# Low parts of expert weights made on GpSimd in the second routing front, and gathers that wait for the token list alone

## The reference, cut to what matters

```python
x = x + attention(layernorm(x))
x = x + mixture_0(layernorm(x))          # 4 experts, hidden 512, one shared expert
x = x + rwkv(layernorm(x))
x = x + mixture_1(layernorm(x))          # 8 experts, hidden 256, biases

# mixture_1
logits = x @ gate_w.T + gate_b
top_vals, top_idx = top_k(logits, 2)
routing = softmax(top_vals)
for e in range(8):
    h = x @ w1[e].T + b1[e]
    y = h[:, 0::2] * sigmoid(1.702 * h[:, 0::2]) * (h[:, 1::2] + 1.0)
    out += (y @ w2[e].T + b2[e]) * sum(routing * (top_idx == e))
```

## Time and profile before

| | |
|---|---|
| median of 3 runs | 743.87 us (743.05 to 746.04) |
| profiled execution, its own time | 742.95 us |
| its span in the trace | 741.1 us |
| PE busy | 660.9 us (89%) |
| DVE busy | 519.2 us (70%) |
| ACT busy | 349.6 us (47%) |
| POOL busy | 338.2 us (46%) |
| second front, from the first instruction to the first `up` | 577.4 to 608.4 us |
| expert phase of the second mixture, from the first `up` | 608.4 to about 714 us |

### The profile page before, as it was taken

The page is one execution under the profiler, slowest core; times in us unless marked ns, Lnnn a source line. Parts: engine busy times, 40 slices in busy tenths (PEclk is TensorE's granted clock), DMA queues, the critical chain, the costliest instruction groups (busy, mean ns, idle before and its releaser), DMA issues. The chain is left out here.

```text
span 741.1 us, 13768 instructions
## 1 busy us (share of the span) xinstructions
PE 660.9 (89%) x4339; PEld 538.2 (73%) x4339; DVE 519.2 (70%) x1087; ACT 349.6 (47%) x735; POOL 338.2 (46%) x326
## 2 busy tenths in 40 slices
PE   8889999889899999999994799999998589999950
PEld 6656666468788888888883688888887257888840
DVE  6778888957854465444442679999883778888847
ACT  2667777736403333333332365555462654555530
POOL 5977777410033433444213245555442065777530
PEclk9999999989999999999998799999987799999985
DMA  6800000110011311111103942000010012333229
GB/s 205 322 1 3 1 2 15 44 34 29 1 35 44 115 51 58 58 53 57 36 29 108 354 152 98 1 0 1 30 53 33 0 54 81 99 98 101 80 80 309
DMA packets 37186, 54.23 MB, mean 73 GB/s; under 512 B 6645, under 2 KB 28919, under 8 KB 36983
## 3 DMA queue, kind: packets, MB, share of 16 engines
q1 hardware_dynamic: 27832, 31.78, 12.8%
q0 software_dynamic: 7104, 19.41, 8.3%
q10 hardware_dynamic: 2176, 2.10, 0.9%
HBM read 37.28 MB, written 15.99 MB: 72 GB/s over the span
## 5 line engine op out<-in xcount | busy, mean ns | idle before, releaser
L1888 PE MATMUL banks<-r_xt,r_w_mixed 128*128 128x256 f32 x384 | 87.6, 388 | 1.4 <-ACT r_xt L1980 1.4
L1888 PEld LDWEIGHTS banks<-r_xt,r_w_mixed 128*128 128x128 f32 x384 | 73.9, 194 | 12.7 <-ACT r_xt L1980 2.1
L1567 DVE SCALAR_TENSOR_TENSOR f0x_s<-f0x_th,banks 128x512 f32<-128x512 f32 x35 | 24.1, 688 | 83.1 <-ACT f0x_th L1526 83.1
L1427 POOL DMA_INDIRECT f_y<-f0x_yout,f_slot_of x35 | 34.6, 987 | 99.4 <-ACT f0x_yout L1542 99.4
L1413 POOL DMA_INDIRECT f0x_xg<-f_xn,f_token_of x35 | 35.0, 999 | 66.0 <-DVE f_slot_of L1045 49.5
L1526 ACT ACTIVATE f0x_th<-banks 128x512 f32<-128x512 f32 x35 | 21.0, 600 | 86.8 <-PE banks L1478 86.8
L659 DVE TENSOR_REDUCE a_ssum<-a_e 128x6 f32<-128x1536 f32 x32 | 56.0, 1748 | 3.8 <-ACT a_e L526 3.6
L1478 PE MATMUL banks<-f_w_hi,f0x_xt_hi 128*128 x140 | 55.4, 396 | 0.9 <-ACT f0x_xt_hi L1517 0.9
L1478 PE MATMUL banks<-f_w_lo,f0x_xt_hi 128*128 x140 | 55.6, 397 | 0.0
L1413 POOL DMA_INDIRECT f1x_xg<-f_xn,f_token_of x39 | 40.8, 1045 | 32.4 <-DVE f_slot_of L1045 19.3
L1478 PE MATMUL banks<-f_w_hi,f0x_xt_lo 128*128 x140 | 55.2, 394 | 0.0
(11 more groups left out here) (357 smaller groups left out, 1885.4 us busy)
## 6 DMA issues: line engine op xcount, KB each, us to landing
f_w_lo<-in_f_w13T SPq DMA_DIRECT2D x4, 2048.0 KB, 12.0
r_y<-f_y SPq DMA_DIRECT2D x16, 256.0 KB, 5.2
f_w_lo<-in_f_w2T SPq DMA_DIRECT2D x4, 512.0 KB, 15.0
f_xn<-f_rows_normed SPq DMA_DIRECT2D x8, 256.0 KB, 2.1
f_b<-in_f_b SPq DMA_DIRECT2D x1, 2048.0 KB, 9.8
f_w_lo<-in_f_w2T SPq DMA_DIRECT2D x2, 1024.0 KB, 11.6
f_xn<-r_y SPq DMA_DIRECT2D x8, 256.0 KB
f1c_y<-f_y SPq DMA_DIRECT2D x8, 256.0 KB, 7.3
```

The source lines that it names most:

```text
L1427: pool.indirect_dma_start(k.y_dram, bass.IndirectOffsetOnAxis(ap=k.slot_of[:, done:done + 1], axis=0), yout[:, done % YB, :], None).then_i ...
L1567: dve.scalar_tensor_tensor(out=s1[:, t % 2, :], in0=th[:, t % 2, :], scalar=1.0, in1=glu_part, op0=ALU.add, op1=ALU.mult).then_inc(s1_done, 1)
L1888: last = pe.matmul(bank(1 + kind)[:, eb * T:(eb + 1) * T], r.w_mixed[:, kind, j // KB, j % KB, eb * P:(eb + 1) * P], xt[:, b % 2, j % KB, ...
```

## The change

In the second front the low parts of the four down units, and of the first three of the eight up units, become GpSimd subtractions of 128 x 1024 numbers, in front of the gathers in GpSimd's queue. TensorE's `take_left`, the negated identity and ScalarE's copies out of PSUM go. VectorE keeps five up units (3 to 7). `weigh` moves from the end of VectorE's queue to a place behind `experts`. `rows` is cut into `tokens` and `slots`, with one low unit (3) between the two and four behind. TensorE gets products whose result nobody reads (`keep_clock`), 14 behind the counts and 8 behind the lists. In both mixtures the gathers wait for `tokens_known` and `planed`, and `slots_known` is waited for in front of the first scatter. In the first front the order of VectorE's steps stays.

```diff
+        k.tables_read = (self.planed, 1)
...
-    def rows(self):
+    def tokens(self):
         dve.wait_ge(t.named, 1)
         then(dve.tensor_scalar(k.token_of[:], t.named_psum, float(TOK), None, ALU.add))
+        k.tokens_known = (t.step, self.done)
+
+    def slots(self):
         then(dve.scalar_tensor_tensor(out=t.unused[:], ...
         dve.wait_ge(t.planed, 1)
...
-        k.rows_known = (t.step, self.done)
+        k.slots_known = (t.step, self.done)
...
-    AT_ROWS, BEFORE_LIST = 2, 2
+    ON_SIDE, BEFORE_SLOTS = 3, 4
+    k.up_known = ((k.hi_done, k.up_parts), (side_low, ON_SIDE), (k.lo_done, k.up_parts - ON_SIDE))
...
     def _(pool):
         rank.clear(pool)
-        pool.memset(neg_ident[:], 0.0).then_inc(neg_zero, 1)
-        pool.wait_ge(neg_zero, 1)
-        pool.affine_select(out=neg_ident[:], ...
+        for n, (hi, lo) in enumerate(down_parts):
+            pool.wait_ge(down_high, n + 1)
+            pool.tensor_tensor(lo, f32(lo), f32(hi), ALU.subtract).then_inc(down_low, 1)
+        for n in range(ON_SIDE):
+            hi, lo = parts[n]
+            pool.wait_ge(k.hi_done, n + 1)
+            pool.tensor_tensor(lo, f32(lo), f32(hi), ALU.subtract).then_inc(side_low, 1)
...
     def _(pe):
+        def keep_clock(times):
+            for _ in range(times):
+                pe.matmul(m.banks[:, 7, 0:2 * P], m.ones[:], m.neg_half[:, 0:2 * P], start=True, stop=True)
         rank.count(pe)
-        pe.wait_ge(neg_ready, 1)
-        for n in range(BEFORE_LIST):
-            take_left(n)
+        keep_clock(14)
         rank.list(pe)
-        for n in range(BEFORE_LIST, len(down_parts)):
-            take_left(n)
+        keep_clock(8)
...
     def _(act):
         down_to_high(2)
-        down_to_low(0)
         down_to_high(3)
-        take_high(0)
-        down_to_low(1)
+        for n in range(4):
+            take_high(n)
         rank.negate(act)
-        for n in range(1, 5):
+        for n in range(4, k.up_parts):
             take_high(n)
-        down_to_low(2)
-        for n in range(5, k.up_parts):
-            take_high(n)
-        down_to_low(3)
...
     def _(dve):
         steps.experts()
-        for n in range(AT_ROWS):
+        steps.weigh()
+        steps.tokens()
+        for n in range(ON_SIDE, BEFORE_SLOTS):
             take_low(dve, n)
-        steps.rows()
-        for n in range(AT_ROWS, k.up_parts):
+        steps.slots()
+        for n in range(BEFORE_SLOTS, k.up_parts):
             take_low(dve, n)
-        steps.weigh()
...
-        pool.wait_ge(*k.rows_known)
+        pool.wait_ge(*k.tokens_known)
+        pool.wait_ge(*k.tables_read)
...
+                if done == 0:
+                    pool.wait_ge(*k.slots_known)
                 pool.wait_ge(y_done, done + 1)
...
                 if t == 0:
-                    pe.wait_ge(k.hi_done, k.up_parts)
-                    pe.wait_ge(k.lo_done, k.up_parts)
+                    for semaphore, value in k.up_known:
+                        pe.wait_ge(semaphore, value)
```

More of the change, by code:

```diff
@@ L1039, in rows @@
         then(dve.tensor_scalar(k.token_of[:], t.named_psum, float(TOK), None, ALU.add))
+        k.tokens_known = (t.step, self.done)
+    def slots(self):
+        t, dve, then, k = self.t, self.dve, self.then, self.k
         then(dve.scalar_tensor_tensor(out=t.unused[:], in0=t.named_psum, scalar=0.0, in1=t.neg_spare[:],
@@ L1075, in first_front @@
     parts, take_low = weight_units(v, k)
+    k.up_known = ((k.hi_done, k.up_parts), (k.lo_done, k.up_parts))
     k.all_known = ((k.hi_done, k.all_parts), (k.lo_done, k.all_parts))
@@ L1266, in second_front @@
     parts, take_low = weight_units(v, k)
-    AT_ROWS, BEFORE_LIST = 2, 2
+    ON_SIDE, BEFORE_SLOTS = 3, 4
     down_parts = parts[k.up_parts:]
-    down_high, down_left, down_low, neg_zero, neg_ready = (
-        sem(n) for n in "down_high down_left down_low neg_zero neg_ready".split())
+    down_high, down_low, side_low = (sem(n) for n in "down_high down_low side_low".split())
+    k.up_known = ((k.hi_done, k.up_parts), (side_low, ON_SIDE), (k.lo_done, k.up_parts - ON_SIDE))
     k.all_known = ((down_high, len(down_parts)), (down_low, len(down_parts)))
-    neg_ident = ctx.enter_context(nc.sbuf_tensor(f"{v.tag}r_neg_ident", [P, P], F32))
-    flat = lambda part: f32(part).rearrange("p e n -> p (e n)")
-    left = lambda n: (m.banks[:, 4:6, :] if n == 1 else m.banks[:, 6:8, :]).rearrange("p b n -> p (b n)")
     @block.gpsimd
@@ L1278, in _ @@
         rank.clear(pool)
-        pool.memset(neg_ident[:], 0.0).then_inc(neg_zero, 1)
-        pool.wait_ge(neg_zero, 1)
-        pool.affine_select(out=neg_ident[:], in_=neg_ident[:], compare_op=ALU.not_equal, fill=-1.0, base=0,
-                           pattern=[[-1, P]], channel_multiplier=1).then_inc(neg_ready, 1)
+        for n, (hi, lo) in enumerate(down_parts):
[5 more added lines that the diff above has]
+            pool.tensor_tensor(lo, f32(lo), f32(hi), ALU.subtract).then_inc(side_low, 1)
     @block.tensor
     def _(pe):
[L1286 to L1293, removed]
-            last.then_inc(down_left, 1)
+        def keep_clock(times):
+            for _ in range(times):
+                pe.matmul(m.banks[:, 7, 0:2 * P], m.ones[:], m.neg_half[:, 0:2 * P], start=True, stop=True)
         rank.count(pe)
-        pe.wait_ge(neg_ready, 1)
-        for n in range(BEFORE_LIST):
-            take_left(n)
+        keep_clock(14)
         rank.list(pe)
-        for n in range(BEFORE_LIST, len(down_parts)):
-            take_left(n)
+        keep_clock(8)
     @block.scalar
```

3 lines of the change are left out of this document (removed).

## The result

The changed kernel takes 751.80 us (median of 4 runs, 751.44 to 752.64), the kernel before 743.46 beside it (4 runs, 742.48 to 746.04). The ratio is 1.0109 with a 95% interval of 1.0084 to 1.0134: slower by about 8.3 us. Forecast were 751.2 us and "slower" as the likeliest case.

What follows compares the result with a forecast made beforehand. The chain of waits up to the first `up` was taken as deciding, with TensorE's expert phase unchanged. Ranking 12.7 us longer, stretch behind it 5.4 shorter: 743.87 + 7.3 = 751.2 us, range 739.0 to 754.5.

Steps and rivals of the forecast that it cites:

- The one number: Start of the first `up`, which all later work follows: forecast at 615.7, 7.3 us later than 608.39.
- What GpSimd gets: Seven subtractions of 128 x 1024 at 2.35 us each, upper bound 2.54, rounded output priced at nothing.
- The hold: In the ranking, GpSimd's SBUF reads hold off VectorE steps with two SBUF inputs, about 2.0 us per larger subtraction.
- The walk: Step-by-step pass through the ranking naming which VectorE steps wait, slip or pass: seven waits, together 12.7 us.
- What goes: Ranking's end to first `up`: `take_left`, ScalarE's copies and three VectorE subtractions go; 16.0 us becomes 10.6, 5.4 less.
- the gathers': Before the first `up`: second gather lands at about 614, before VectorE's last unit at 615.1, so costs nothing.
- The clock: TensorE's granted clock around the first `up`: 0 added, 1.5 us kept for the range if first tiles run at half speed.
- A: Rival: the two engines don't hinder one another; first `up` 5.1 us sooner, 4.6 put, 739.3 us; chance 0.29.
- B: Rival: the wait doesn't grow with subtraction size; 5.8 us on the ranking, time about 744; chance 0.13.
- C: Same mechanism in full: 2.54 us subtractions held to the end, 3.1 more plus clock 1.5, 754 to 756; within likeliest case's 0.58.
- The page's rule: SBUF contention between VectorE and GpSimd: whoever issues second is blocked fully; to the letter, about 2 us more.

Runs made afterwards that it cites:

- experiment 1: The changed kernel with the seven GpSimd subtractions waiting until the ranking's tables are written: 753.36 us, ratio 1.0136 to the kernel before.
- experiment 2: The changed kernel with each GpSimd subtraction replaced by two memsets, which read nothing (low parts zero): 739.40 us, ratio 0.9953 to the kernel before.
- experiment 3: The changed kernel with each GpSimd subtraction replaced by a one-input copy (low parts wrong): 742.53 us, ratio 0.9997 to the kernel before.
- 4: The changed kernel with each GpSimd subtraction cut into two of 128 x 512: 749.03 us, ratio 1.0080 to the kernel before.
- 5: The changed kernel with only the four down units on GpSimd and all eight up units on VectorE: 748.52 us, ratio 1.0065 to the kernel before.
- 7: The kernel before with only the gathers' wait changed, to the token list and the plane instead of the slots: 742.72 us, ratio 0.9995.
- 9: The kernel before, reworked with no low part on GpSimd; VectorE subtracts the fourth down unit in its wait for first `up`: 739.79 us with unread products, 740.23 without.
- experiment 6: The changed kernel without both calls of `keep_clock`, the products nobody reads: 752.83 us, ratio 1.0131 to the kernel before.

## Why the prediction was right, point by point

- **The one number.** The first `up` was forecast at 615.7 and came at 617.38, the median at 751.2 and came at 751.80. TensorE's work behind it is unchanged, as said. That the median is only 0.6 us off is partly luck. The first `up` came 1.7 us later than forecast; the trace took 0.5 us less behind it, within what the same work varies, and the kernel before measured 743.46 beside the changed one, where the forecast started from 743.87.
- **What GpSimd gets.** 2.35 us a subtraction, predicted and measured; the rounded output format costs nothing. The first starts at 579.95 (forecast 579.7).
- **The hold.** Right in kind, and shown by five experiments: it goes with the subtractions when they move (1), vanishes for steps with two inputs when GpSimd doesn't read (2), shrinks with a shorter read (3, 4), and scales with their number (5). The size was forecast as 12.7 us in seven waits of 1.6 to 2.0; it is 13.69 in seven waits of 1.70 to 2.11 (the held duration less the step's own). One piece of evidence for it was read too neatly. Rows 8 show gathers of 1.9 us beside VectorE's subtractions and one of 0.95 without, but the next two in the same trace, at 603.15 and 604.40, also meet VectorE's subtractions (603.44 to 606.94) and take 0.95 and 1.08.
- **The walk.** Its detail was wrong. I let one step with two inputs slip through each gap between subtractions, and named L973, L976, L993, L996, L998, L1000, L1006 as held. Held were L973, L974, L993, L994, L996, L998 and L999 in the numbering of before, one directly behind the other where no reduction stands between: nothing slips. So four of the seven named steps were held, and the three that were to slip were held too. L976, L1000 and L1006 passed, since GpSimd was idle at that moment: waiting for the third high copy, or through at 599.4. The sum held up because the number of waits is the number of subtractions, whichever step each of them hits; that it did so with the wrong steps was luck.
- **What goes.** 10.6 us were forecast from the ranking's end to the first `up`, 11.1 measured. VectorE's part was right: its last unit ends 9.7 us behind the ranking (four from 611.36 in 4.63 us: 615.99), forecast 10.0. The term at fault is the gathers', put at nothing. The second was said to land at about 614, 1.1 us before VectorE's last unit. With the ranking ending 1.2 us later than forecast that is 615.2; it landed at 616.35, behind the last unit. One cause is its issue at 612.67, where 610.8 + 1.2 = 612.0 was forecast: the first gather does not follow the token list (known at 609.5) but starts 0.8 us behind the plane's list (610.5), as in the kernel before (7), and it is issued at 611.30. The other is the time from issue to landing. The 3.2 us were read from the end of the data's movement; in the traces TensorE turns the second tile 3.7 us behind its issue (3.68 here, 3.68 and 3.69 in the two versions of 9), and both belong to an issue of 1.85 to 1.88 us.
- **The clock.** Put at 0 with 1.5 in the range, and the clock was full at the first `up`. The way there was not the one forecast. The eight products were to take 0.2 to 0.4 us each, with a wait of 2 to 3 us behind them; they take 5.76 us in all (sixteen records, two for each), end at 616.07, and hold back the first tile by 1.7 us without holding back the first `up`. The fourteen take 8.05 us, forecast 3 to 6. Without both calls the first tiles run at half clock and about 1 us is lost, as 6 shows by its trace.
- **The rivals.** A was right for its own condition. It had the first `up` 5.1 us sooner and put 4.6; experiment 2, less its 1.8 us of waits, has it 4.8 us sooner, and on the scale of the forecast that is 743.87 x 0.9953 - 1.8 = 738.6 us, against 739.3. B's time (about 744) is that of experiment 3, where the waits are 0.62 us on average. C's sum has a slip: 2.54 - 2.0 is 0.54 and not 0.45, so its seven waits add 3.8 us and it ends near 756.5.
- **The page's rule.** Read to the letter, the Trainium skill, SBUF — State Buffer, section "Who interferes with whom", would have added about 2 us to the sum; the 13.69 lie between my 12.7 and that. The longest hold, 2.11 us of a subtraction of 2.33, is of the step that was ready 0.10 us behind the subtraction's start (592.49 against 592.39). The same section of the Trainium skill says that casts and tensor_scalar can take both ports and that a reduction never does. The rows of experiment 1 agree (1.80 to 2.33 us against 0.48 for the reduction), and so does experiment 2, where even a memset holds the casts and not the steps with two inputs. I had used only the half of the rule on two inputs.

## What to carry to other kernels

An idle engine isn't free capacity if its reads hold off the engine that carries the chain. Count, for every instruction put on GpSimd beside a chain of short dependent VectorE steps, one wait of a good part of its length, however small the VectorE step is: 1.7 to 2.1 us for a subtraction of 2.35, 0.4 to 0.8 for a copy of 1.04. Ask first whether VectorE has a wait of its own, in which the work costs nothing. Here there were 1.7 us in front of the first bias addition, and the fourth down unit went into them at no loss that the trace shows (9). When the path is shortened by more than a microsecond or two, walk the next one too: here the second gather's data came 0.4 us behind the last unit, and the first `up` some 0.9 us late for it.

## What the runs showed of the hardware that was not expected

- VectorE's casts and tensor_scalars from SBUF to SBUF wait for GpSimd as the steps with two inputs do (2.33 us in the place of 0.18 beside a subtraction), and also beside a memset, which reads nothing (0.98 us). In the second fronts of these runs reductions (0.29 to 0.48 us), the reciprocal (0.25) and steps that read PSUM (0.18 to 0.29) were never held.
- GpSimd's one-input copy of 128 x 1024 takes 1.04 us and its memset 0.95, against 2.35 for the subtraction.
- The issue of a gather mostly takes 1.85 to 1.96 us beside VectorE's subtractions and 0.95 without them, as in the earlier trace rows, in the changed kernel too. It is not so for every one: 0.95 and 1.08 were seen beside them in the kernel before, 1.06 in the changed one. GpSimd seems to be held by VectorE also where it only prepares a transfer. In experiment 6 the tile whose issue took 1.06 us (from 611.17) was turned 3.1 us behind the start of its issue, the one whose issue took 1.88 us (from 612.54) 3.7 us. So a short issue would bring the second gather some 0.6 us sooner, an estimate from these two; it was not tried.
